# The write of a unit's shifted scores as two transfers of 64 partitions, in a relative-position attention kernel

## The chip, the cores and the metric

The kernel runs on one core of a Trainium2 chip. The metric is the device time of one execution in microseconds. The core has a matrix engine (PE, with its weight loads shown as PEld), a vector engine (DVE), a scalar engine (ACT), a general engine (POOL) and a queue engine (SP) that only issues transfers. ACT issues transfers too. The transfers of both run on the same 16 DMA engines of the core; the profile calls the queue of SP q1 and that of ACT q10.

## The reference

For 16 batches of 512 tokens of width 128 the kernel computes x + attention(LN(x)) + MLP(LN(x)). The attention has 16 heads of width 8 and relative positions; its core, for each batch and head, is:

```
content = einsum(q + u_bias, k)           # 512 x 512 per head
pos     = einsum(q + v_bias, p)           # 512 x 512 per head
# relative shift: a zero column is put ahead, and the rows of 513 are
# read again as rows of 512, from the second row on
padded  = concat([zeros(S, 1), pos])      # 512 x 513
pos     = padded.reshape(S + 1, S)[1:]    # 512 x 512
attn    = softmax((content + pos) * scale)
head    = attn @ v
```

All data are float32. The MLP has three layers with weights of plus and minus one.

## The kernel before

A *unit* is one head of one batch: 256 units. Time is laid out by hand in *halves*, two for each unit. Every engine walks over the same sequence of halves, and semaphores join the engines. The stages of unit u are:

1. Halves 2u to 2u+3: PE multiplies position scores into PSUM (`positions`, L779). ACT copies 128x1024 of them a half into `pos_sb` (L463), whose rows are 513 wide with a zero in the first column. There are four buffers of `pos_sb`.
2. After the copy of half 2u+3, SP writes the unit's `pos_sb` to the DRAM buffer `shift` (L307): 128 partitions of 2052 floats, 1026 KB. This waits for the copies (`s_pe`) and, as there are six buffers of `shift`, for the load of the unit six earlier (`s_in`).
3. At half 2u+8, ACT waits for the write (`s_out_w`, of which there is one for each `pos_sb` buffer) and for a free buffer of `sc_sb`, and issues the load of the same bytes, read from an offset of 512 floats on, into `sc_sb` (L450): this write and read make the relative shift. The wait is in ACT's own sequence. While it is open, the copies and exponentials behind it stand.
4. From half 2u+12, PE multiplies the content scores, DVE adds the loaded shifted scores (L630) and subtracts the row's extreme (L638).
5. From half 2u+17, PE turns the scores (L803) and ACT takes the exponential (L473), then PE multiplies with the values (L817).

The DRAM side of the write is the view `chunks`: element (q, a, c) with 32 q, 4 a and 2052 c; partition p of `pos_sb` holds q = p // 4 and a = p % 4. Between the units' work stand *jobs* (projections, MLP, output), placed by the tables `FRONT`, `MIDDLE` and `BACK`. SP's sequence has, beside one write for each unit, one load of x and one store of the output for each batch. The sequence repeats every 16 units.

Of the kernel before, what the change touches and what calls it, by code (L numbers as in the profile page):

```python
# [11 lines left out]
P = 128  # L12
# [5 lines left out]
def attention_mlp(nc, x, consts, stack_w, wp, pe_t, k0, k1, k2, out):  # L18
# [18 lines left out]
    N_POS = 4  # L37
    N_SC = 6
    N_SHIFT = 6
# [3 lines left out]
    shift = nc.dram_tensor("shift", [N_SHIFT, S * PITCH], F32, kind="Internal").ap()  # L43

    with ExitStack() as ctx:
        def sb(name, shape, dt=F32):
            return ctx.enter_context(nc.sbuf_tensor(name, shape, dt))
# [4 lines left out]
        def sem(name):  # L52
            return ctx.enter_context(nc.semaphore(name))
# [49 lines left out]
        pos_sb = sb("pos_sb", [P, N_POS, NT, PITCH])  # L103
# [47 lines left out]
        s_out_w = [sem(f"s_pout{i}") for i in range(N_POS)]  # L151
# [12 lines left out]
        def wait(eng, s, n):  # L164
            if n > 0:
                eng.wait_ge(s, n)
# [34 lines left out]
        def taken(h):  # L201
            return [j[:3] for j in AT.get(h, []) if j[3] == j[4] - 1]
# [13 lines left out]
        def ev(name, b, c=0):  # L216
            return EV[(name, b, c)] if b >= 0 else 0
# [12 lines left out]
        def unit(n, lag):  # L230
            return n - lag if 0 <= n - lag < UNITS else None

        def half_of(h, lag):
            k = h - lag
            return divmod(k, 2) if 0 <= k < 2 * UNITS else (None, None)

        def blocks(h, lag):

            u, i = divmod(h - lag, 2)
            return [(v, t) for v, t in ((u - 1, i + 2), (u, i)) if 0 <= v < UNITS]  # L240
# [4 lines left out]
        def score_halves(h):  # L245

            return min(max(h + 1, 0), 2 * UNITS + 2)
# [3 lines left out]
        def pt_banks(k):  # L251
            return ps_pos if k >= TWO_PT and (k - TWO_PT) % 2 == 0 else ps_pt
# [16 lines left out]
        def chunks(flat):  # L269

            return flat.rearrange("(a q c) -> q a c", a=4, q=P // 4)
# [6 lines left out]
        @block.sync  # L278
        def _(sp):
            def load_x(b):  # L280
                wait(sp, s_out, 16 * (b - N_X + 1))
                sp.dma_start(x_sb[:, b % N_X].rearrange("p t d -> p (t d)"), chunks(x[b].rearrange("s d -> (s d)"))) \
                  .then_inc(s_x[b % N_X], 16)

            load_x(0)
            sp.dma_start(wp_sb[:, :], wp).then_inc(s_wp, 16)
            sp.dma_start(pe_sb[:, :], pe_t).then_inc(s_enc, 16)
            sp.dma_start(wk, stack_w[:, GROUPS * P:2 * GROUPS * P]).then_inc(s_wk, 16)
            for dst, src in ((k0_u8, k0), (k1_u8, k1), (k2_u8, k2)):
                sp.dma_start(dst, src.rearrange("(a p) n -> p a n", p=P)).then_inc(s_wb, 16)  # L290
            load_x(1)

            for n in STEPS:
                it, slot = n // 16, n % 16
                if it >= 2 and slot == 1:
                    sp.wait_ge(s_jev, ev("TY", it - 2))
                    sp.dma_start(chunks(out[it - 2].rearrange("s d -> (s d)")),
                                 x_sb[:, (it - 2) % N_X].rearrange("p t d -> p (t d)")).then_inc(s_out, 16)
                if 0 <= it and it + 2 < B and slot == 4:
                    load_x(it + 2)  # L300
                u = unit(n, 1)
                if u is not None:
                    sp.wait_ge(s_pe, score_halves(2 * u + 3))
                    if u >= N_SHIFT:
                        v = u - N_SHIFT
                        sp.wait_ge(s_in[v % N_SC], 16 * (v // N_SC + 1))
                    sp.dma_start(chunks(shift[u % N_SHIFT]),  # L307
                                 pos_sb[:, u % N_POS].rearrange("p t c -> p (t c)")) \
                      .then_inc(s_out_w[u % N_POS], 16)
            for k in range(2):  # L310
                sp.wait_ge(s_tail["x"], k + 1)
                sp.dma_start(chunks(out[B - 1].rearrange("s d -> (s d)"))[:, :, 2 * k * D:2 * (k + 1) * D],
                             x_sb[:, (B - 1) % N_X, 2 * k:2 * k + 2, :].rearrange("p t d -> p (t d)")) \
                  .then_inc(s_out, 16)
            sp.wait_ge(s_out, 16 * (B + 1))
# [71 lines left out]
        def _(act):  # L387
# [57 lines left out]
            for h in HALVES:  # L445
                u, i = half_of(h, SHIFT_H)
                if i == 0:
                    act.wait_ge(s_out_w[u % N_POS], 16 * (u // N_POS + 1))
                    wait(act, s_pt, 2 * (u - N_SC + 1))
                    act.dma_start(sc_sb[:, u % N_SC].rearrange("p t c -> p (t c)"),  # L450
                                  chunks(shift[u % N_SHIFT, S:S + S * S])) \
                       .then_inc(s_in[u % N_SC], 16)
                todo = sorted(blocks(h, 0), key=lambda v: v[0] % N_POS)
                if todo:
                    act.wait_ge(s_pos, score_halves(h))
                    for u, t in todo:
                        if t == 0 and u >= N_POS:
                            act.wait_ge(s_out_w[u % N_POS], 16 * (u // N_POS))
                    to = [pos_sb[:, u % N_POS, t, 1:PITCH] for u, t in todo]
                    if len(to) == 2:  # L460
                        to = bass.AP(tensor=to[0].tensor, offset=to[0].offset,
                                     ap=[to[0].ap[0], [to[1].offset - to[0].offset, 2], [1, S]])
                        act.copy(to, ps_pos[:, :, :]).then_inc(s_pe, 1)  # L463
                    else:
                        act.copy(to[0], ps_pos[:, 0, :]).then_inc(s_pe, 1)
                u, i = half_of(h, TURN_H)
                if u is not None:
                    k = 2 * u + i
                    act.wait_ge(s_pt, k + 1)
                    if k == 0:  # L470
                        act.wait_ge(s_wf, 3)
                    wait(act, s_av, k - 1)
                    act.activation(pt_sb[:, 2 * i:2 * i + 2, :], pt_banks(k)[:, :, :], ACT.Exp, scale=-1.0) \  # L473
                       .then_inc(s_exp, 1)
                for j in taken(h):
                    take_job(*j)
                for name, b, c in taken(h - 1):
                    if name == "TZ" and b > 0:
                        act.wait_ge(s_jev, ev("TZ", b))
                        act.copy(z_t[:, :].rearrange("d (a q t) -> d t q a", a=4, t=NT),  # L480
                                 z_q[:, :].rearrange("d (t q a) -> d t q a", a=4, t=NT)).then_inc(s_zt, 1)
# [432 lines left out]
```

## Time and profile before

| | |
|---|---|
| runs | 1458.58, 1460.66, 1461.72 us; median 1460.66 |
| profiled execution | 1460.97 us, of which the span of instructions is 1459.2 us |
| granted clock of PE, mean | 0.999 of full speed |
| bytes moved by DMA | 550.41 MB |

The difference between the execution's time and its span, 1.8 us, lies before the first and after the last instruction. In the section of rows below, a busy time is a sum over instructions. The DMA share is the time in which a packet was open, over the 16 engines; it says little about how much more they could carry, which the GB/s beside it tell better. "To landing" is from the issue of a transfer to its completion.

### The profile page before, as it was taken

Reading aid. Unit: us, or ns where it says so; the run is one execution under the profiler, and the core shown is the slowest. Engines: PE = TensorE matmul, PEld = TensorE weight load, DVE = VectorE, ACT = ScalarE, POOL = GpSimd, SP = SyncE. Lnnn points to the kernel's source line nnn. Section 1 sums busy time; section 2 is a strip of 40 time slices with the busy share of each in tenths; the row PEclk is TensorE's granted clock in tenths of the full one; section 3 lists DMA queues with packets and bytes.
Section 4 is the critical chain, followed back from the end, with each engine's and each line's share of the span. In section 5 each row is a group of like instructions: output and inputs, shape, how many; then the busy total and the mean of one; then the engine's idle time right before and its main releaser. Section 6 shows DMA issues by size and latency. Waiting matters only on the chain.

```text
span 1459.2 us, 41448 instructions
## 1 busy us (share of the span) xinstructions
PE 1444.7 (99%) x16113; PEld 961.4 (66%) x16113; DVE 1335.9 (92%) x3490; ACT 1225.5 (84%) x1364; POOL 726.4 (50%) x721
## 2 busy tenths in 40 slices
PE   8999999999999999999999999999999999999998
PEld 5566666666666666666666666666766666666666
DVE  6899899999999999999998999999899998989996
ACT  5788888888888888888888888888888888888873
POOL 5555455454654556455554555456455554533410
PEclk9999999999999999999999999999999999999999
DMA  5999999999999999999999999999999999999992
GB/s 175 407 397 399 386 391 384 381 394 384 394 381 392 398 383 396 376 391 384 390 397 382 400 384 390 393 375 403 382 391 394 384 398 385 393 381 388 388 403 92
DMA packets 80867, 550.41 MB, mean 377 GB/s; under 512 B 9376, under 2 KB 10528, under 8 KB 15136
## 3 DMA queue, kind: packets, MB, share of 16 engines
q1 hardware_dynamic: 43376, 278.61, 49.3%
q10 hardware_dynamic: 37296, 269.15, 47.9%
q8 instruction: 129, 2.11, 0.6%
q14 instruction: 66, 0.54, 0.1%
HBM read 274.57 MB, written 273.15 MB: 375 GB/s over the span
## 4 chain that ended last, share of the span: by engine, by line
PE 93%; DMA 4%; ACT 2%; DVE 1%; issue 1%; ACTq 0%
PE ps_pt L803 34%; PE ps_av L817 18%; PE ps_pos L779 14%; PE ps_job L706 12%; DMA shift<-pos_sb 4%; PE ps_job L663 3%; PE ps_job L670 3%; PE ps_job L685 2%; ACT pt_sb L473 1%; PE ps_job L681 1%; PE ps_job L693 1%; PE ps_job L676 1%; PE ps_con L791 1%; PE ps_av L655 1%; ACT pos_sb L463 1%
## 5 line engine op out<-in xcount | busy, mean ns | idle before, releaser
L630 DVE CUSTOM_DVE_ANT_0 sc_sb<-ps_con,sc_sb 128x512 f32<-128x512 f32 x1024 | 662.5, 683 | 89.7 <-PE ps_con L791 85.7
L463 ACT COPY pos_sb<-ps_pos 128x1024 f32<-128x1024 f32 x510 | 518.4, 1016 | 190.2 <-PE ps_pos L779 181.1
L638 DVE TENSOR_SCALAR sc_sb<-sc_sb,nmax 128x512 f32<-128x512 f32 x1024 | 604.7, 622 | 0.1
L803 PE MATMUL ps_pt<-c_sb,sc_sb 128*128 128x128 f32 x4048 | 552.5, 279 | 3.4 <-ACT pt_sb L473 2.3
L473 ACT ACTIVATE pt_sb<-ps_pt 128x1024 f32<-128x1024 f32 x506 | 519.5, 1027 | 14.0 <-PE ps_pt L803 13.7
L803 PEld LDWEIGHTS ps_pt<-c_sb,sc_sb 128*128 128x128 f32 x4048 | 433.2, 141 | 128.1 <-issue 96.7
L817 PE MATMUL ps_av<-pt_sb,v_sb 128*9 128x128 f32 x8192 | 319.9, 274 | 0.6 <-ACT pt_sb L473 0.6
L817 PEld LDWEIGHTS ps_av<-pt_sb,v_sb 128*9 128x9 f32 x8192 | 172.8, 90 | 208.3 <-issue 205.5
L366 POOL CAST h<-act_sb 128x512 fp32r<-128x512 f32 x128 | 83.0, 649 | 390.8 <-ACT act_sb L439 390.4
L791 PE MATMUL ps_con<-k_stack,q_stack 26*128 26x512 f32 x1024 | 261.9, 496 | 0.1
L779 PE MATMUL ps_pos<-p_stack,q_stack 26*128 26x512 f32 x1024 | 258.5, 496 | 3.4 <-ACT pos_sb L463 3.0
L706 PE MATMUL ps_job<-h,w 128*128 128x512 f32 x640 | 188.9, 417 | 0.0
L779 PEld LDWEIGHTS ps_pos<-p_stack,q_stack 26*128 26x128 f32 x1024 | 96.7, 181 | 118.4 <-issue 110.8
L367 POOL TENSOR_TENSOR h<-act_sb,h 128x512 fp32r<-128x512 f32 x128 | 164.3, 1283 | 10.4
L357 POOL TENSOR_TENSOR k_stack<-act_sb,c_sb 128x512 fp32r<-128x512 f32 x63 | 70.4, 1118 | 122.3 <-ACT act_sb L434 122.3
L357 POOL TENSOR_TENSOR q_stack<-act_sb,c_sb 128x512 fp32r<-128x512 f32 x62 | 69.5, 1122 | 114.7 <-ACT act_sb L434 114.0
L706 PEld LDWEIGHTS ps_job<-h,w 128*128 128x128 f32 x640 | 108.6, 190 | 15.2 <-ACT act_sb L434 0.2
L791 PEld LDWEIGHTS ps_con<-k_stack,q_stack 26*128 26x128 f32 x1024 | 98.4, 181 | 4.1 <-DVE nmax L630 2.4
L439 ACT ACTIVATE act_sb<-ps_job,col 128x512 f32<-128x512 f32 x128 | 87.8, 686 | 1.8 <-PE ps_job L706 1.7
L358 POOL TENSOR_TENSOR k_stack<-act_sb,k_stack 128x512 fp32r<-128x512 f32 x63 | 80.6, 1279 | 4.9
L630 DVE DVE_READ_ACCUMULATOR2_ANT nmax<- 128x1 f32 x1024 | 81.9, 80 | 0.0
L358 POOL TENSOR_TENSOR q_stack<-act_sb,q_stack 128x512 fp32r<-128x512 f32 x62 | 79.4, 1281 | 4.9
(109 smaller groups left out, 983.2 us busy)
## 6 DMA issues: line engine op xcount, KB each, us to landing
shift<-pos_sb SPq DMA_DIRECT2D x256, 1026.0 KB, 9.2
sc_sb<-shift ACTq DMA_DIRECT2D x256, 1024.0 KB, 9.9
x_sb<-in_x SPq DMA_DIRECT2D x16, 256.0 KB, 10.9
out<-x_sb SPq DMA_DIRECT2D x15, 256.0 KB, 10.1
c_sb<-in_consts ACTq DMA_DIRECT2D x1, 288.0 KB, 6.9
o_t<-in_wp SPq DMA_DIRECT2D x1, 256.0 KB, 5.5
stack_w_sb<-in_stack_w ACTq DMA_DIRECT2D x1, 256.0 KB, 5.1
heads<-in_pe_t SPq DMA_DIRECT2D x1, 256.0 KB, 6.6
```

What stands on the lines that cost most here:

```text
L357: own(pool.tensor_tensor(dst, src, low.broadcast_to([P, S]), ALU.mult))
L358: pool.tensor_tensor(dst, src, dst.bitcast(F32), ALU.subtract).then_inc(s_hl, 1)
L367: pool.tensor_tensor(dst[:, 1, :], src, dst[:, 0, :].bitcast(F32), ALU.subtract) \
L463: act.copy(to, ps_pos[:, :, :]).then_inc(s_pe, 1)
L473: act.activation(pt_sb[:, 2 * i:2 * i + 2, :], pt_banks(k)[:, :, :], ACT.Exp, scale=-1.0) \
L630: dve.tensor_tensor_reduce(sc_sb[:, m % N_SC, t, :], ps_con[:, k, :], sc_sb[:, m % N_SC, t, :], -SCALE, 3.4e38, ALU.add, ALU.min, nmax[:, ...
L638: dve.tensor_scalar(sc_sb[:, m % N_SC, t, :], sc_sb[:, m % N_SC, t, :], nmax[:, m % N_SC, t:t + 1], None, ALU.subtract).then_inc(s_sub, 1)
L706: return pe.matmul(ps_job[:, :], lhs, src[:, a, hl, :], start=(a == 0 and hl == 0), stop=(a == len(before) - 1 and hl == 1))
L779: ins = pe.matmul(ps_pos[:, bank, :], QS[rows, g, t * P:(t + 1) * P], PS[rows, g, :], start=True, stop=True)
L791: pe.matmul(ps_con[:, bank, :], QS[rows, g, t * P:(t + 1) * P], KS[rows, g, :], start=True, stop=True).then_inc(s_con, 1)
L803: last = pe.transpose(pt_banks(k)[:, j % 2, t * P:(t + 1) * P], sc_sb[:, u % N_SC, t, j * P:(j + 1) * P], id_sb)
L817: last = pe.matmul(ps_av[32 * t:32 * t + DH + 1, h % 4, :], v_sb[:, b % 2, j, h, :], pt_sb[:, j, t * P:(t + 1) * P], start=(j == 0), stop= ...
```

## The change

SP issues two transfers for a unit where there was one. The first takes partitions 0 to 63 of `pos_sb` to the first 16 of 32 q of the DRAM view, the second partitions 64 to 127 to the other 16. The bytes and their places are the same. Both add 16 to the same semaphore, so the two waits of ACT on it (ahead of the load, and ahead of the reuse of a `pos_sb` buffer) ask for 32 for each use.

```diff
                         sp.wait_ge(s_in[v % N_SC], 16 * (v // N_SC + 1))
-                    sp.dma_start(chunks(shift[u % N_SHIFT]),
-                                 pos_sb[:, u % N_POS].rearrange("p t c -> p (t c)")) \
-                      .then_inc(s_out_w[u % N_POS], 16)
+                    for k in range(2):
+                        sp.dma_start(chunks(shift[u % N_SHIFT])[P // 8 * k:P // 8 * (k + 1)],
+                                     pos_sb[P // 2 * k:P // 2 * (k + 1), u % N_POS].rearrange("p t c -> p (t c)")) \
+                          .then_inc(s_out_w[u % N_POS], 16)
...
-                    act.wait_ge(s_out_w[u % N_POS], 16 * (u // N_POS + 1))
+                    act.wait_ge(s_out_w[u % N_POS], 32 * (u // N_POS + 1))
...
-                            act.wait_ge(s_out_w[u % N_POS], 16 * (u // N_POS))
+                            act.wait_ge(s_out_w[u % N_POS], 32 * (u // N_POS))
```

SP's queue, at the place in the first third of a batch where a store of the output and a load of x stand between the writes; before (`s_pe` is ACT's copies, `s_in` the load of six units earlier, `s_jev` and `s_out` belong to the output):

```order
L307 DMA shift<-pos_sb 32x4x2052 [waits s_in1,s_pe]
L297 DMA out<-x_sb 32x4x512 [waits s_jev]
L307 DMA shift<-pos_sb 32x4x2052 [waits s_in2,s_pe]
L307 DMA shift<-pos_sb 32x4x2052 [waits s_in3,s_pe]
L307 DMA shift<-pos_sb 32x4x2052 [waits s_in4,s_pe]
L282 DMA x_sb<-in_x 128x1x512 [waits s_out]
```

The same place of the changed kernel:

```order
L308 DMA shift<-pos_sb 16x4x2052 [waits s_in1,s_pe]
L308 DMA shift<-pos_sb 16x4x2052
L297 DMA out<-x_sb 32x4x512 [waits s_jev]
L308 DMA shift<-pos_sb 16x4x2052 [waits s_in2,s_pe]
L308 DMA shift<-pos_sb 16x4x2052
L308 DMA shift<-pos_sb 16x4x2052 [waits s_in3,s_pe]
L308 DMA shift<-pos_sb 16x4x2052
L308 DMA shift<-pos_sb 16x4x2052 [waits s_in4,s_pe]
L308 DMA shift<-pos_sb 16x4x2052
L282 DMA x_sb<-in_x 128x1x512 [waits s_out]
```

Each write has become two with half the q, the second of which waits for nothing; no other transfer has changed its place between units. ACT's sequence in the middle of a batch, where it waits for the writes (`s_pout2` is the `s_out_w` of one `pos_sb` buffer), before:

```order
L450 DMA sc_sb<-shift 128x1x2048 [waits s_pt,s_pout2]
L463 COPY pos_sb<-ps_pos 128x2x512 [waits s_pout2,s_pos]
L473 ACTIVATE pt_sb<-ps_pt 128x1024 [waits s_av,s_pt]
L463 COPY pos_sb<-ps_pos 128x2x512 [waits s_pos]
L473 ACTIVATE pt_sb<-ps_pt 128x1024 [waits s_av,s_pt]
```

And of the changed kernel:

```order
L451 DMA sc_sb<-shift 128x1x2048 [waits s_pt,s_pout2]
L464 COPY pos_sb<-ps_pos 128x2x512 [waits s_pout2,s_pos]
L474 ACTIVATE pt_sb<-ps_pt 128x1024 [waits s_av,s_pt]
L464 COPY pos_sb<-ps_pos 128x2x512 [waits s_pos]
L474 ACTIVATE pt_sb<-ps_pt 128x1024 [waits s_av,s_pt]
```

Only the line numbers and the counts that are waited for have moved. The orders of PE, DVE and POOL are the same as well.

## Rows read from the trace of the kernel before

**Rows 1.** Page, part 1: busy time and share of each engine.

```profile
PE 1444.7 (99%) x16113; PEld 961.4 (66%) x16113; DVE 1335.9 (92%) x3490; ACT 1225.5 (84%) x1364; POOL 726.4 (50%) x721
```

**Rows 2.** Page, part 4: the chain that ended last, by engine.

```profile
PE 93%; DMA 4%; ACT 2%; DVE 1%; issue 1%; ACTq 0%
```

**Rows 3.** Windows of three batches: length, busy (count), clock, DMA share, GB/s.

```profile
1077.14:1165.01 87.87, 87.87 (x1007) 58.75 (x1004) 81.98 (x216) 76.37 (x85) 47.14 (x47) 1.00 1.01 387
1165.01:1252.88 87.87, 87.87 (x1006) 58.75 (x1004) 82.00 (x216) 76.37 (x85) 47.19 (x47) 1.00 1.01 393
1252.88:1340.74 87.86, 87.86 (x1004) 58.74 (x1004) 81.60 (x208) 76.37 (x85) 39.72 (x38) 1.00 1.01 386
```

**Rows 4.** Waits of the SP queue: us in total, times, longest.

```profile
SPq L307 <- ACT pos_sb L463: 1234.4, 255, 13.4
```

**Rows 5.** Waits of all engines, whole span.

```profile
ACT pos_sb L463 <- PE ps_pos L779: 181.1, 366, 1.2
...
ACT pos_sb L463 <- DMA shift<-pos_sb: 3.2, 1, 3.2
...
DVE sc_sb L630 <- DMA sc_sb<-shift: 2.9, 3, 1.4
```

**Rows 6.** Chain in order of time, its long DMA pieces: start us, us, what.

```profile
34.47 11.25 DMA shift<-pos_sb
...
206.68 13.53 DMA shift<-pos_sb
...
295.07 13.74 DMA shift<-pos_sb
...
647.95 13.65 DMA shift<-pos_sb
```

**Rows 7.** DMA issues: KB each, median us to landing.

```profile
shift<-pos_sb SPq DMA_DIRECT2D x256, 1026.0 KB, 9.2
sc_sb<-shift ACTq DMA_DIRECT2D x256, 1024.0 KB, 9.9
...
out<-x_sb SPq DMA_DIRECT2D x2, 128.0 KB, 2.1
```

**Rows 8.** Line L307, window 60 to 1400: issue durations in ns, landing.

```profile
L307 SPq DMA_DIRECT2D shift<-pos_sb x244: 517/518/532, 60.6 to 1396.3; - x122
...
DMA to landing us min/median/max: 6.7/9.2/13.7
```

**Rows 9.** Line L307, window 19 to 22: the first write, alone.

```profile
L307 SPq DMA_DIRECT2D shift<-pos_sb x1: 587/587/587, 20.1 to 20.1; - x1
...
DMA to landing us min/median/max: 4.4/4.4/4.4
```

**Rows 10.** Line L307, window 704 to 706: a write in mid-run.

```profile
L307 SPq DMA_DIRECT2D shift<-pos_sb x1: 517/517/517, 704.6 to 704.6; - x1
...
DMA to landing us min/median/max: 9.2/9.2/9.2
```

**Rows 11.** Timeline of ACT: that write's load is issued.

```profile
716.18 0.52 ACTq L450 DMA_DIRECT2D sc_sb<-shift  x1
```

**Rows 12.** Timeline of ACT around 220 us.

```profile
220.23 0.52 ACTq L450 DMA_DIRECT2D sc_sb<-shift  x1
220.85 1.02 ACT L463 COPY pos_sb<-ps_pos 128x1024 f32<-128x1024 f32 x1 [1.44 <-PE ps_pt L803]
```

**Rows 13.** Window 34 to 60, columns as in rows 3.

```profile
34.00:60.00 26.00, 22.86 (x117) 12.74 (x116) 20.99 (x51) 16.47 (x20) 15.35 (x15) 0.93 1.01 405
```

**Rows 14.** Line L307, window 1415 to 1416: the last write.

```profile
DMA to landing us min/median/max: 11.0/11.0/11.0
```

**Rows 15.** Line L450, window 1426 to 1428: its load.

```profile
L450 ACTq DMA_DIRECT2D sc_sb<-shift x1: 521/521/521, 1426.5 to 1426.5; - x1
```

**Rows 16.** Page, part 3: packets, MB and share of each queue.

```profile
q1 hardware_dynamic: 43376, 278.61, 49.3%
q10 hardware_dynamic: 37296, 269.15, 47.9%
```

## The prediction, made before the changed kernel was run

> **What bounds the kernel now.** I read the share of each engine first [rows 1]: PE is busy for 99% of the span, DVE for 92%, ACT for 84%. The chain that ended last [rows 2] is 93% PE and 4% DMA. Windows laid over three batches [rows 3] agree: 87.87 us each, of which PE works 87.87 us at full clock. That is 5.49 us for each of 16 units. So in mid-run PE is the bound, and a change on a transfer can only save what is lost outside of such batches.
>
> Then the transfers, since the change is one of them. SP has time: it waits 1234 us in all, 255 times, for ACT's copies [rows 4], and an issue takes it 0.52 us [rows 8]. The transfer itself has little. The write of a unit is issued after the copy of half 2u+3 and must have landed when ACT comes to half 2u+8. In mid-run it was issued at 704.6 and landed 9.2 us later, at 713.8 [rows 10]. ACT issued the load at 716.18 [rows 11], so 2.4 us were left. The landing times reach from 6.7 to 13.7 us [rows 8], and the slack is often gone. Of the 256 pairs of a write and its load, worked out in this way, 31 have the load within 0.3 us of the write's landing. The first is the write issued at 34.47 with a landing of 11.25 us [rows 6], the last the one at 1415.4, which landed after 11.0 us and whose load went out at 1426.5 [rows 14, 15]. 47 pairs have under 1 us, 100 under 2 us. Most of the short ones cost nothing yet, since ACT has about 0.7 us of idle time a unit (181.1 us of waits for PE [rows 5], over 256). Four are on the chain [rows 6]: the one at 34.47, where ACT's next copy stood 3.2 us for it [rows 5], and three of 13.5 to 13.7 us. At the one that landed at 220.2, ACT's copy had been idle for 1.44 us [rows 12], about 1 us more than usual.
>
> Why a write takes 9.2 us is told by comparing it with one that is alone. The first write landed in 4.4 us [rows 9]; one of 128 KB at the end takes 2.1 us [rows 7]. The difference, 898 KB in 2.3 us, is 400 GB/s. So the bytes of one write stream for 2.63 us, and some 1.8 us are fixed. In mid-run a write and a load share the engines. How near are these to their limit? In the stretch of 34 to 60 us, where ACT was waiting for writes and PE was idle for 3 us, they moved 405 GB/s [rows 13]; in the PE-bound batches 387 to 393 [rows 3], 389 in the mean. 389 GB/s over 5.49 us is 2.13 MB for a unit; at 405 GB/s this takes 5.27 us, which is just two times 2.63. **The DMA engines would bound the kernel at 5.27 us a unit, and PE does at 5.49: the cover is 0.22 us, 4%.**
>
> **The change, part by part.**
>
> *One more issue for each unit.* 256 more instructions on SP, each 0.52 us [rows 8]. SP is idle 1234 us of 1459, so SP itself is not late. The second half starts some 0.55 us after the first. With one more write or load still on the queues, as is the rule (9.2 us to land against a unit's 5.49), the engines have the first half to move meanwhile (1.3 us at full rate), so this costs nothing in mid-run. For a write that finds the engines idle it costs up to 0.5 us; only the first two do, and neither is waited for. The out store and the x load behind the writes are 0.55 us later, with a batch's time to spare. Zero.
>
> *16 more completion packets a unit.* q1 has 43376 packets, q10 37296 [rows 16]. For 256 writes this fits 128 packets of data and 16 of completion each. The change makes that 128 + 32, and the queue's total 47472. What a completion packet costs is not seen by itself. The backlog's 405 GB/s, which carries two sets of completions a unit, is no lower than the 400 GB/s that come from data alone, so the lower bound is nothing. For the upper bound I give all of the fixed 1.8 us to the completions of a transfer and let no other packet pass meanwhile, which no row suggests: 1.8 us a unit. I take 0, nearer to the two equal rates.
>
> *Each transfer touches 64 partitions.* This is where the price lies. The first write shows a transfer that reads all 128 partitions: 400 GB/s. No row has a transfer of 64. If the paths by which the DMA engines reach the on-chip memory are spread over the partitions, half of the partitions offer half of the paths, and with one half read after the other, the unit's write streams for 2.63 f us, where f is between 1 (the path is no limit) and 2 (it always is). With f = 2 the write alone takes 5.26 us, with the load's 2.63 behind it 7.9 us. But f falls where engines alternate between a write packet and a load packet: two engines that share a path collide only while both are at a write. In perfect alternation f is 1, with chance phases about 1.4. I take f = 1.2, the middle of these two, as nearer to the only rows there are, in which a write and a load run side by side without loss (2 x 2.63 = 5.27). A unit then needs 2.63 + 2.63 x 1.2 = 5.79 us on the DMA engines. This is above PE's 5.49: **the bound moves from PE to DMA, and each unit is 0.30 us longer**. The break-even is f = 1.09.
>
> The Trainium skill speaks on this. Its page "SBUF — State Buffer", section "Door 1: The DMA port swizzle", says that partitions 0 to 63 reach only 8 of 16 ports, and gives 196 GB/s for them at 1 MiB against 328 for all 128. By these figures an estimate for a unit's write is 5.4 us against 3.2, f = 1.7, if nothing of it were hidden behind the load. No run here shows a half transfer; the trace agrees as far as 128 partitions alone ran above what the page gives for 8 ports. The page "DMA: Bandwidth & Descriptors", section "Rules for kernel authors", advises against this very split, as the halves run one after the other.
>
> *The counts of 32.* They make ACT wait for both halves, so nothing is released sooner. Zero.
>
> **Sum.** The own time of the profiled execution is 1460.97 us. From 60 to 1400 us there are 244 units [rows 8]: 244 x 0.30 = +73. The stretch of 34 to 60 us, already held by DMA, has 5 units at +0.53 = +2.6. The three steps of about 1 us at the late writes go up in the new period, -3. Total +73, or 1534 us. The execution lies 0.3 us above the median of the runs shown, which is nothing here.
>
> **The rivals.**
>
> *DMA latency rises, but PE stays the bound.* If f is below 1.09, the transfers still fit, with 0 to 0.2 us of cover left, and writes land perhaps 0.5 to 1 us later. For it: 47 pairs have under 1 us. Against a large price: ACT's idle 0.7 us a unit takes up most overruns. Some ten more stalls of 1 to 1.5 us, +4 to +15: about 1470 us.
>
> *Hidden altogether.* If all 16 engines read the halves at full rate and the second issue stands behind the first, writes land as before. For it: SP's idle time, the backlog. Against: it needs both the path and the completions free with 4% to spare. 1461 us, within 3.
>
> *Faster.* Mechanism: with two shorter transfers each engine's part is in smaller runs, and if the first half's fixed 1.8 us passes under the second's streaming, the last byte lands earlier by a part of it. It decides if the landing falls by about 1 us: then the write at 34.47 no longer holds ACT's copy (-3.2 us) and the three mid-run steps go (-3). More cannot be had, since the batches are PE's. 1455 us. Against it: the fixed time is paid after the last byte, which no split moves forward, and the last half is issued later.
>
> *The rule of the ports in full.* f at chance phases or above, 1.4: 6.31 us a unit, +0.82 x 244 = +200: 1660 us. For it are the first page's figures only; in the rows nothing. It lies at the end of the first case.
>
> **How the numbers follow.** DMA becomes the bound: 0.47, its own range 1475 to 1640 (f from 1.1 to 1.37). Latency only: 0.20. Hidden: 0.18. Faster: 0.15. A measurement of this kernel can tell about 0.2% (3 us) from no change. Slower by more: 0.47 + 0.19 = 0.66; same: 0.01 + 0.17 + 0.02 = 0.20; faster: 0.01 + 0.13 = 0.14. The range for 8 in 10 must take in both signs: 1457 leaves out most of the faster case, 1610 the cases of f above 1.32.
>
> **What would show it.** In the changed kernel's profile: the first write, alone, lands after 6 us or more instead of 4.4 if half the partitions mean half the rate; after 5.0 if only the second issue counts. The landing of the halves' second in mid-run goes from 9.2 to above 11 us. Batches are longer than 87.87 us with PE idle, the long pieces of the write stand all along the chain, and the waits gain a large row of ACT's copy for the write. GB/s falls to about 370 with the engines' share still at 1.0. SP's idle time stays above 1000 us. I am wrong if the batches keep their 87.87 us and landings their median.

## The result, and the profile of the changed kernel

The changed kernel takes 1479.49 us (1477.79 to 1481.75), the kernel before 1461.19 us on the same chip: a ratio of 1.013, with a 95% interval of 1.0108 to 1.0151. It is slower, as forecast, but by 18 us and not by 73. The profiled execution took 1481.08 us with a span of 1479.2 us. One execution of one kernel further down ("More time before ACT's wait", with one transfer) ran at a granted clock of 0.556 and took 2377 us; it is left out of every time given here.

Page of the changed kernel: busy time by engine, then the chain by engine, then two rows of the transfers.

```profile
PE 1450.8 (98%) x16113; PEld 964.5 (65%) x16113; DVE 1338.6 (90%) x3490; ACT 1224.2 (83%) x1364; POOL 722.6 (49%) x721
...
q1 hardware_dynamic: 47472, 278.63, 49.9%
...
PE 87%; DMA 8%; ACT 2%; DVE 1%; issue 1%; SPq 0%; ACTq 0%
...
sc_sb<-shift ACTq DMA_DIRECT2D x256, 1024.0 KB, 10.4
```

The engines do the same work as in [rows 1]. On the chain DMA has 8% instead of 4% [rows 2]. The packets of SP's queue are the 47472 that were forecast, against [rows 16].

Windows of 88 us through the first part of the run (length, busy times, clock, DMA share, GB/s):

```profile
60.00:148.00 88.00, 87.01 (x987) 57.40 (x986) 79.28 (x208) 75.82 (x84) 46.52 (x46) 0.99 0.99 382
148.00:236.00 88.00, 85.62 (x979) 57.05 (x976) 80.17 (x207) 74.28 (x83) 44.27 (x44) 1.00 1.00 381
236.00:324.00 88.00, 86.74 (x982) 58.07 (x981) 81.20 (x214) 75.05 (x85) 45.14 (x46) 1.00 1.00 383
324.00:412.00 88.00, 88.00 (x1008) 58.78 (x1010) 82.17 (x216) 76.28 (x86) 46.56 (x47) 1.00 1.01 389
412.00:500.00 88.00, 85.05 (x957) 56.57 (x956) 78.00 (x203) 72.01 (x81) 42.63 (x43) 0.98 1.00 372
500.00:588.00 88.00, 88.00 (x1011) 58.73 (x1002) 82.10 (x216) 76.48 (x86) 46.83 (x46) 1.00 1.00 388
```

This is the row that the forecast got wrong. Some windows are still wholly PE's, at 388 and 389 GB/s as in [rows 3]. Others lack 1 to 3 us of PE. So the period did not become longer everywhere; it is broken at single places. The prediction named the opposite as its sign: batches longer throughout and about 370 GB/s. The lowest of these windows has 372, the undisturbed ones 388 and 389. The chain names them, to be read against [rows 6]:

```profile
37.38 10.68 DMA shift<-pos_sb
...
197.04 13.83 DMA shift<-pos_sb
...
287.39 12.72 DMA shift<-pos_sb
...
465.55 13.74 DMA shift<-pos_sb
...
645.31 12.29 DMA shift<-pos_sb
...
749.90 13.27 DMA shift<-pos_sb
...
1000.40 12.89 DMA shift<-pos_sb
...
1178.22 12.95 DMA shift<-pos_sb
...
1410.65 11.42 DMA shift<-pos_sb
```

Nine where there were four. Six of the seven that lie in mid-run (all but the one at 749.90) are the write that SP issues next after a batch's output store; the seventh stands behind the load of x. From 60 us on, the 14 writes behind an output store land after 12.6 us in the mean, where the kernel before has 9.9; the 221 writes with neither the store nor the load of x directly ahead take 10.8 against 9.3. So the late ones come about once a batch, where a 256 KB store shares the queue.

The waits say the same; before it was 3.2 us, once [rows 5]. First all engines, then SP's queue, where 1234.4 us [rows 4] have become 1010.3:

```profile
ACT pos_sb L464 <- DMA shift<-pos_sb: 18.2, 9, 3.6
```

```profile
SPq L308 <- ACT pos_sb L464: 1010.3, 255, 14.5
```

The largest of these steps, on ACT's timeline (the load is issued at 479.31, 2.6 us after ACT was free, and the copy behind it had stood for 3.21 us):

```profile
476.04 0.68 ACT L440 ACTIVATE act_sb<-ps_job,col 128x512 f32<-128x512 f32 x1
479.31 0.52 ACTq L451 DMA_DIRECT2D sc_sb<-shift  x1
479.93 1.01 ACT L464 COPY pos_sb<-ps_pos 128x1024 f32<-128x1024 f32 x1 [3.21 <-DMA shift<-pos_sb]
```

Paired one by one, a unit's write (from the first issue to the landing of the last half) takes 10.9 us in the mean against 9.4, and its load 10.4 against 9.9. The median of the write is 10.8; the prediction's sign was above 11. The time left before ACT issues the load has fallen from a median of 2.2 us to 0.9, and pairs with under 0.3 us are 73 instead of 31. (Both halves count on one semaphore, so the landing given for a first half can be made up of completions of the second. With a tiny transfer on the same semaphore, an experiment below, the whole write seemed to land at a median of 7.0 us instead of 9.2. Only the last landing of a unit is used here.)

Where the 20 us of the span arise follows from the times at which the write of the same unit is first issued in the two traces. At unit 0 the changed kernel is 0.7 us late, which has nothing to do with the change; at unit 8 it is 5.6 us late and at unit 32 as well; at 64, 128, 192 and 255 it is 7.8, 12.5, 16.5 and 19.9 us late. So 5 us are lost in the start, up to 60 us, and 14 us in mid-run, in steps of up to 5 us.

The traces also record every packet. A write's packet is 8208 bytes. In the first write, which is alone, it is open for 470 ns in the mean against 315 before. From 324 to 1200 us it is open for 344 ns against 337, and a packet of the load for 335 against 339. Each engine carries 8 of both kinds a unit, which makes 5.43 us of open time against 5.41. So alone the packets of a half get in each other's way, and in the mixed stream hardly anything of it shows in their times.

### The profile page after: what moved, and what is told of

Its sections match the earlier page's. It is cut to its first block, busy times and chain, and to the rows that moved or that the text cites. A ratio compares the mean times of both kernels' runs of the same rounds, so it can differ in the third digit from the quotient of the medians.

```text
span 1479.2 us, 41704 instructions
## 1 busy us (share of the span) xinstructions
PE 1450.8 (98%) x16113; PEld 964.5 (65%) x16113; DVE 1338.6 (90%) x3490; ACT 1224.2 (83%) x1364; POOL 722.6 (49%) x721
## 3 DMA queue, kind: packets, MB, share of 16 engines
q1 hardware_dynamic: 47472, 278.63, 49.9%
## 4 chain that ended last, share of the span: by engine, by line
PE 87%; DMA 8%; ACT 2%; DVE 1%; issue 1%; SPq 0%; ACTq 0%
PE ps_pt L804 32%; PE ps_av L818 17%; PE ps_pos L780 13%; PE ps_job L707 11%; DMA shift<-pos_sb 8%; PE ps_job L671 4%; PE ps_job L664 3%; ACT pt_sb L474 1%; PE ps_job L686 1%; PE ps_job L682 1%; PE ps_job L694 1%; PE ps_job L677 1%; ACT pos_sb L464 1%; PE ps_av L656 1%; PE ps_con L792 1%
## 5 line engine op out<-in xcount | busy, mean ns | idle before, releaser
L780 PE MATMUL ps_pos<-p_stack,q_stack 26*128 26x512 f32 x1024 | 259.2, 496 | 12.6 <-ACT pos_sb L464 12.2
L368 POOL TENSOR_TENSOR h<-act_sb,h 128x512 fp32r<-128x512 f32 x128 | 164.6, 1286 | 10.4
## 6 DMA issues: line engine op xcount, KB each, us to landing
sc_sb<-shift ACTq DMA_DIRECT2D x256, 1024.0 KB, 10.4
```

The lines of the kernel that those rows point to most:

```text
L368: pool.tensor_tensor(dst[:, 1, :], src, dst[:, 0, :].bitcast(F32), ALU.subtract) \
L780: ins = pe.matmul(ps_pos[:, bank, :], QS[rows, g, t * P:(t + 1) * P], PS[rows, g, :], start=True, stop=True)
```

## The experiments

All ratios are to the kernel before on the same chip, with 95% intervals. **Theory A**: a transfer that covers a contiguous half of the partitions reaches memory by fewer paths. **Theory B**: the second issue and the completions cost the time.

**Even and odd partitions.**

```diff
-                        sp.dma_start(chunks(shift[u % N_SHIFT])[P // 8 * k:P // 8 * (k + 1)],
-                                     pos_sb[P // 2 * k:P // 2 * (k + 1), u % N_POS].rearrange("p t c -> p (t c)")) \
+                        sp.dma_start(chunks(shift[u % N_SHIFT])[:, k::2, :],
+                                     pos_sb[k::2, u % N_POS].rearrange("p t c -> p (t c)")) \
```

> Two transfers of 64 partitions for each unit as in the changed kernel, but the first takes the even partitions and the second the odd ones (32 q of 2 a). Issues, packets, their sizes and completions are those of the changed kernel. Theory A (a contiguous half of the partitions is reached by fewer paths): the cost goes away, 1461 within 4 us, mid-run landing of a unit's write back near 9.4 us, first unit's write alone landed about 5.0 us after its first issue instead of 6.0. Theory B (the second issue and the 16 more completions cost it): the time stays at 1479 within 4 us, and the first write still takes about 6.0 us.

Measured: 1459.2 us, ratio 0.9989 (0.9980 to 0.9998). The first unit's write, alone, in this kernel:

```profile
L308 SPq DMA_DIRECT2D shift<-pos_sb x2: 589/594/599, 19.9 to 20.6; - x2
...
DMA to landing us min/median/max: 3.1/3.5/3.8
```

and in the changed kernel:

```profile
L308 SPq DMA_DIRECT2D shift<-pos_sb x2: 590/592/595, 20.8 to 21.4; - x2
...
DMA to landing us min/median/max: 4.4/4.9/5.4
```

Even and odd: 20.6 + 3.8 = 24.4, which is 4.5 us after the first issue, as fast as the one transfer of [rows 9]. Contiguous halves: 21.4 + 5.4 = 26.8, 6.0 us. Issues, packets and completions are equal, and a packet of the even/odd kernel's first write is open for 315 ns, as in the kernel before. So the cost lies in which partitions and rows a half takes, as theory A has it, and theory B falls. Each half still has 64 partitions: it is not their number that costs. Paired, the mid-run write takes 9.6 us. The edit changes the DRAM side too, which the next two kernels take apart.

**Which side of the transfer?** Two mirrored kernels: one has the DRAM view of the even/odd kernel with the on-chip view of the changed one, the other the reverse. In both the rows of `shift` are permuted, so the scores are other numbers; nothing else is left out.

```diff
-                        sp.dma_start(chunks(shift[u % N_SHIFT])[P // 8 * k:P // 8 * (k + 1)],
+                        sp.dma_start(chunks(shift[u % N_SHIFT])[:, k::2, :],
```

```diff
-                                     pos_sb[P // 2 * k:P // 2 * (k + 1), u % N_POS].rearrange("p t c -> p (t c)")) \
+                                     pos_sb[k::2, u % N_POS].rearrange("p t c -> p (t c)")) \
```

> On-chip side as in the changed kernel (partitions 0 to 63, then 64 to 127), DRAM side as in the even/odd kernel (32 q of 2 a). The rows of shift are permuted by this, so the scores are other numbers; nothing else is left out. Theory A1 (the on-chip partitions' paths cost it): as the changed kernel, 1475 to 1482 us. Theory A2 (the DRAM side of the halves costs it): 1459 to 1462 us.

> The mirror of the run before: on-chip side even and odd partitions, DRAM side as in the changed kernel (16 q of 4 a, then the other 16), again with permuted rows. Theory A1: 1458 to 1462 us. Theory A2: 1475 to 1482 us.

Measured: contiguous on chip alone 1481.36 us, ratio 1.0115 (1.0066 to 1.0164), in the range of the changed kernel's 1.013. Contiguous in DRAM alone 1474.58 us, ratio 1.0045 (1.0016 to 1.0073); on this chip the kernel before took 1466.0 us, and the ratio is what counts. (The first one's trace is of its slowest execution, 1487.17 us of 1478.23 to 1487.17.) Waits of ACT's copy for the write, of the first, then of the second:

```profile
ACT pos_sb L464 <- DMA shift<-pos_sb: 29.4, 17, 3.4
```

```profile
ACT pos_sb L464 <- DMA shift<-pos_sb: 14.0, 8, 3.0
```

The first unit's write, alone, of the first and of the second:

```profile
L308 SPq DMA_DIRECT2D shift<-pos_sb x2: 588/593/598, 20.3 to 20.9; - x2
...
DMA to landing us min/median/max: 4.4/5.1/5.8
```

```profile
L308 SPq DMA_DIRECT2D shift<-pos_sb x2: 583/589/595, 20.2 to 20.9; - x2
...
DMA to landing us min/median/max: 4.1/4.4/4.8
```

That is 6.4 us for contiguous halves on chip alone and 5.4 us (5.38 before rounding) for contiguous halves in DRAM alone, against 4.5 for even and odd on both sides and 6.0 for contiguous on both. The mean time for which a packet of it is open is 549, 417, 315 and 470 ns in the same order. So the on-chip side carries most of the time lost, but the second kernel is far from free: it was expected to cost nothing, costs 0.45%, and its paired writes in mid-run land after 10.9 us in the mean, as late as the changed kernel's. Either the DRAM side has a price, or the other pairing of partitions with rows has one; no run separates these. It also shows that the mean landing does not fix the loss: with the same 10.9 us, 89 of its pairs have under 0.3 us, and it loses a third as much.

**One tiny transfer more.**

```diff
                       .then_inc(s_out_w[u % N_POS], 16)
+                    sp.dma_start(spare[u % N_POS], pos_sb[0:16, u % N_POS, 0, 0:16]) \
+                      .then_inc(s_out_w[u % N_POS], 16)
```

> The kernel before with one more transfer behind each write, 16 partitions of 16 floats into a spare buffer, on the same semaphore (so ACT waits for 32 as in the changed kernel): one more issue and 16 more completions a unit, next to no bytes. The big write is whole. Theory A: 1461 to 1465 us. Theory B: near 1479 us, and the landing of a unit's writes up by 1.5 us as in the changed kernel.

Measured: 1466.8 us, ratio 1.0041 (1.0017 to 1.0065). So an issue, 16 packets of 64 bytes and 16 completions behind the whole write cost 6 us, more than nothing. From the write's issue to the tiny transfer's landing it is 10.4 us in the mean, 0.9 above the kernel before. They are last on the queue and ACT waits for them:

```profile
ACT pos_sb L466 <- DMA spare<-pos_sb: 10.0, 6, 1.9
```

The even/odd kernel has as many and loses nothing, so this is not a third of the changed kernel's loss that could be added up.

**Halves of the columns.**

```diff
+                        sp.dma_start(chunks(shift[u % N_SHIFT])[:, :, 2 * PITCH * k:2 * PITCH * (k + 1)],
+                                     pos_sb[:, u % N_POS, 2 * k:2 * k + 2].rearrange("p t c -> p (t c)")) \
```

> Two transfers of all 128 partitions and half the columns (1026 floats each): the same issues and completions a unit as the changed kernel, twice the data packets at half the size (4104 bytes). Theory A: 1461 to 1466 us, the rest above the kernel before being the price of 128 more packets a unit. Theory B: 1479 or more.

Measured: 1665.25 us, ratio 1.1375 (1.1324 to 1.1426). Theory A's 1461 to 1466 is missed, and theory B's "1479 or more" is met in form only: the even/odd kernel has the same issues and completions and loses nothing. A second experiment cuts the load in the same way (and its two waits ask for 32).

```diff
-                    act.dma_start(sc_sb[:, u % N_SC].rearrange("p t c -> p (t c)"),
-                                  chunks(shift[u % N_SHIFT, S:S + S * S])) \
+                    for k in range(2):
+                        act.dma_start(sc_sb[:, u % N_SC, 2 * k:2 * k + 2].rearrange("p t c -> p (t c)"),
+                                      chunks(shift[u % N_SHIFT, S:S + S * S])[:, :, 2 * k * S:2 * (k + 1) * S]) \
```

> The column kernel, which took 1665 us, with the load cut into two column halves as well, so that the packets of the two queues are again about equal (4104 and 4096 bytes). If the write starved because the engines serve the two queues packet by packet and its packets were half as long, the time falls back towards 1470 us. If packets of 4104 bytes to DRAM rows cost the engines themselves, it stays at 1665 us or grows.

Measured: 1596.66 us, ratio 1.0926 (1.0874 to 1.0977). One window of each (500 to 675.7 us), first of the column kernel, then with both cut:

```profile
500.00:675.70 175.70, 157.84 (x1754) 103.67 (x1750) 151.10 (x381) 129.81 (x149) 79.99 (x80) 0.99 1.02 343
```

```profile
500.00:675.70 175.70, 164.30 (x1848) 108.91 (x1847) 152.94 (x396) 136.95 (x157) 81.16 (x83) 0.99 1.05 358
```

This lies between the two outcomes that were expected. Still more packets made it faster, so a part of the first loss was, most likely, the unequal packets of the two queues. But with the engines open all the time both stay at 343 and 358 GB/s, so packets of 4.1 KB cost the engines themselves as well. How much of this is the size and how much that two transfers now write each 8208-byte row of DRAM is open.

**Less computation, so that the transfers bound it.** Three kernels.

```diff
-                return [lambda a=a, hl=hl: product(a, hl) for a in range(len(before)) for hl in range(2)]
+                return [lambda a=a, hl=hl: product(a, hl) for a in range(len(before)) for hl in range(2)
+                        if (a, hl) == (0, 0) or a == len(before) - 1]
...
-                for j in (2 * i, 2 * i + 1):
+                for j in (2 * i,):
...
+                    part = slice(0, S if k == 0 else 64)
-                    dve.tensor_scalar(sc_sb[:, m % N_SC, t, :], sc_sb[:, m % N_SC, t, :],
+                    dve.tensor_scalar(sc_sb[:, m % N_SC, t, part], sc_sb[:, m % N_SC, t, part],
```

> Kernel before with less computation, so that PE needs some 4.6 us a unit, ACT 4.8 and DVE 4.2: 5 of 8 products of each MLP layer-1 and layer-2 job, half of the value matmuls and 7/8 of every second subtraction are left out. All transfers stand. The DMA engines should be the bound: 5.27 us a unit by the backlog's rate, about 1405 us in all, GB/s 405, writes waited for throughout.

> The same omissions in the changed kernel. Its period a unit is the DMA engines' own need with contiguous halves, 2.63 (1 + f). The prediction's f = 1.2 gives 5.79 us. Since the changed kernel lost only 18 us in all, f near 1.06 to 1.09 is as well possible: 5.42 to 5.5 us. If the halves cost latency only and no rate, the period is that of the light kernel before, within 0.05 us.

> The same omissions with even and odd partitions as the two transfers. Theory A (paths): the period of the light kernel before within 0.05 us. Theory B (issues and completions): that of the light changed kernel.

Measured: 1434.04 us (1426.86 and 1441.23), 1453.64 us (eight executions, 1445.45 to 1459.20) and 1438.08 us (1433.97 and 1442.20). The middle window (675.7 to 851.4) of one transfer, and of contiguous halves:

```profile
675.70:851.40 175.70, 163.68 (x1491) 101.43 (x1491) 161.84 (x443) 154.98 (x176) 94.43 (x97) 0.99 1.01 403
```

```profile
675.70:851.40 175.70, 160.34 (x1447) 99.19 (x1446) 157.41 (x432) 149.63 (x171) 91.14 (x92) 0.99 1.01 394
```

Over three such windows each, the means are 397, 390 and 398 GB/s. With 2.13 MB a unit these are periods of 5.37, 5.47 and 5.36 us. Contiguous halves cost 0.10 us a unit here: f = 1 + 0.10 / 2.63 = 1.04, where the prediction had 1.2. Two things make this an estimate only. The traces are of the fastest execution of the first kernel and of the slowest of the second, and by the medians the difference is 20 us over 256 units, 0.08 us a unit with the start's loss in it, or f = 1.03. And the light kernels are not held by DMA alone (25% of the first one's chain, 31% of the second's), so the engines' own need can have grown by more than the period. The packets speak against much more: in mid-run those of the two queues are open for 340 + 333 ns against 331 + 333, 0.07 us a unit. The light kernel with one transfer also did not reach the 1405 us that I expected of it.

**The load cut to a quarter** (the buffer it fills is set to zero at the start).

```diff
-                    act.dma_start(sc_sb[:, u % N_SC].rearrange("p t c -> p (t c)"),
-                                  chunks(shift[u % N_SHIFT, S:S + S * S])) \
+                    act.dma_start(sc_sb[:, u % N_SC].rearrange("p t c -> p (t c)")[:, 0:512],
+                                  chunks(shift[u % N_SHIFT, S:S + S * S])[:, :, 0:512]) \
```

> The kernel before with the load of shifted scores cut to a quarter (512 of 2048 floats of each partition; the rest of the scores stays what it was, and a memset of that buffer at the start adds some us). With little to share the engines with, a write in mid-run should land near what it takes alone: 4.5 to 5 us.

> The same cut in the changed kernel. If the two halves collide with themselves on the paths and are only spared by the alternation with the load's packets, a unit's write now takes about 6 us from the first issue, 1.5 us above the run before, as it does for the first unit, and yet the total is that of the run before within 3 us, since ACT comes for it 11 us after the issue. If instead the load makes the conflict, the difference of the landings shrinks to the 0.6 us of the second issue.

Measured: 1469.14 and 1468.27 us. First the kernel with one transfer, its writes from 60 to 1400 us and a window (the DMA share is the last figure but one); then the same of the halves, with one unit in mid-run:

```profile
DMA to landing us min/median/max: 4.7/5.0/6.5
```

```profile
500.00:675.70 175.70, 175.70 (x2005) 117.49 (x2004) 164.01 (x431) 152.63 (x171) 93.15 (x93) 1.00 0.75 247
```

```profile
L308 SPq DMA_DIRECT2D shift<-pos_sb x2: 518/556/595, 574.1 to 574.6; - x2
...
DMA to landing us min/median/max: 4.9/5.5/6.2
```

```profile
500.00:675.70 175.70, 175.70 (x2007) 117.47 (x2005) 164.15 (x431) 152.71 (x171) 93.31 (x93) 1.00 0.90 247
```

One write lands after 5.0 us; two halves end at 574.6 + 6.2 = 580.8, 6.7 us after 574.1 (median over the run 6.9). For the same 247 GB/s the engines have packets open for 0.90 of the time instead of 0.75. So the halves do collide with themselves, in mid-run too, and with time to spare (4.7 us in the median before the load is issued) this costs the total nothing. The rise of 1.9 us was expected as 1.5.

**More time before ACT's wait.**

```diff
-    SHIFT_H = 8
-    CONTENT_LAG = 6
+    SHIFT_H = 9
+    CONTENT_LAG = 7
...
-    N_POS = 4
+    N_POS = 5
```

> The kernel before with one more half for the write and one more for the load: SHIFT_H 9 instead of 8, CONTENT_LAG 7 instead of 6, five pos_sb buffers instead of four, the last batch's two closing jobs two halves later. To make room, three of four blocks of the MLP's second hidden layer share one place (its numbers are other ones; all instructions stand). A write has about 2.8 us more until ACT waits for it. Before has four such waits on its chain, worth about 6 us; the longer pipeline costs 5.5 us at the end. Some 1460 us, no chain piece of the write in mid-run.

> The same in the changed kernel. Theory A with the price paid at ACT's wait (the halves cost latency and little rate): the loss is gone, the time is that of the run before within 3 us, with landings still 1.5 us above its. If the halves cost rate beyond PE's 5.49 us a unit, the loss stays: about 18 us above the run before.

Measured: 1566.65 and 1573.23 us. Both miss the expected time by 100 us: in the new order PE itself needs 5.9 us a unit (98% of the second kernel's chain), so it is no better kernel. Room for the fifth buffer was made by letting three blocks of the MLP's second hidden layer share one place, and the last batch's closing jobs are two halves later. What it does show: all waits of the second for the write, 5.4 us in two, lie before 60 us, none later, and the halves cost it 6.6 us, about what they cost the changed kernel in its start. That is more than the 3 us expected; that it arises in the start is read from the second kernel's waits alone. Its waits for the two transfers:

```profile
ACT pos_sb L465 <- DMA shift<-pos_sb: 5.4, 2, 3.3
DVE sc_sb L632 <- DMA sc_sb<-shift: 5.0, 1, 5.0
```

The transfers also run at a lower rate here (361 GB/s in mid-run), so more time and less load together took the mid-run loss away; which of the two did it is not separated.

## Why the prediction was right in direction and wrong in size

**The bound before** was read rightly. PE holds the batches, the DMA engines have a few per cent to spare, and the write's landing is the thin place.

**Each transfer touches 64 partitions**: half right. The halves do slow each other, and the first write alone needs 6.0 us, which was the sign named for it. But the reason given was that half of the partitions offer half of the paths, and the even/odd kernel also has 64 partitions a transfer and loses nothing. What costs is the contiguous half, on chip most, and on the DRAM side or by the pairing too (5.4 us alone), which the prediction did not consider. That fewer paths are behind it remains an inference from longer packets (470 against 315 ns); no run shows the paths.

**The step that failed is the value f = 1.2**, and with it "the bound moves from PE to DMA, and each unit is 0.30 us longer". It was the middle between perfect alternation (1) and chance phases (1.4), and neither 1.4 nor the choice of the middle came from a row. In the light kernels it is about 1.03 to 1.04, and the packets of the changed kernel itself are open for only 0.02 us more a unit, which as an estimate is 1.01; all are below the break-even of 1.09 that the text itself gave. Alone, f is (6.0 - 1.8) / 2.63 = 1.6, so the collisions are strong when a write has the engines to itself, and nearly gone in rate where a load runs beside it. The +73 of 244 equal units was therefore no term at all. (The case's own lower end was also off: f = 1.1 gives 5.52 us, which is +8 and 1469 us, not 1475. And its "rule of the ports in full", 1660 us, lies outside its range and got no chance.) In its place stands what the first rival described, with a larger price: landings 1.5 us later, nine late writes on the chain instead of four, 14 us in mid-run. The measured 1479.49 us falls into the range of the favoured case by number, 1475 to 1640, but not by its mechanism. I gave this rival 0.20 and +4 to +15 us, the price too low because I let ACT's 0.7 us of idle time absorb most overruns. It does at 64 of the 73 pairs without slack; the other nine cost up to 5 us each. What the prediction left out is where they come: it treated all units alike, and six of the seven in mid-run stand behind the batch's output store, where a write now takes 12.6 us. PE then stands as well, and in the window from 412 to 500 its mean granted clock is 0.98.

**The start** had +2.6 us for the stretch already held by DMA. It is about 5 us. The even/odd kernel also loses 1.6 us there, so not all of it is the contiguous halves.

**One more issue for each unit** was put at nothing, at 0.52 us each. It is not quite that. Issues of the changed kernel last up to 2.5 us in mid-run. At the worst late write the first half's issue took 1.18 us, behind an output store whose issue took 2.87:

```profile
459.74 2.87 SPq L297 DMA_DIRECT2D out<-x_sb  x1
```

```profile
L308 SPq DMA_DIRECT2D shift<-pos_sb x1: 1184/1184/1184, 464.3 to 464.3; - x1
```

SP has time for this in general, but there it came on top of a landing of 13.7 us. It is not the rule: in five of the seven late writes of mid-run the second half was issued 0.56 us after the first, and in two 1.1 to 1.2 us after. With the load cut to a quarter, issues last up to 2.6 us and nothing is lost. So long issues are not the main cause; whether they add something at those two is not separated.

**The completions** at nothing: borne out by the even/odd kernel and by the packets (a completion is open for 9 ns), though a tiny transfer at the end of the queue is not free (+6 us).

**The counts of 32** and the orders of the other engines: as forecast, nothing. **Faster** did not occur for the changed kernel. For even and odd partitions the ratio's interval ends just below 1; by the 0.2% bound it is no change, and no run here that does all the work beats the kernel before by more.

## What to carry to other kernels

When a transfer is split, split it so that each part still spans the partitions evenly, let both sides of it take the same rows, and keep its packets long. The half that is contiguous in partitions took 6.0 us instead of 4.4 alone, the half in columns cost 14%, the even/odd one nothing. And when a resource with 4% to spare gets 2% more work, do not multiply a longer period by all units: pair each issue with its landing, see how the slack is distributed, and look at what else stands in the queue where it is short.

## What the runs showed of the hardware that was not expected

- Two transfers of all partitions with packets of 4104 bytes instead of one with 8208 took the rate in mid-run from 386 to 393 GB/s down to 332 to 343 with the engines open throughout, and shortening the other queue's packets as well brought some of it back (358 to 360 GB/s).
- A DMA's partitions may be strided on the on-chip side (every second one) at no cost: 4.5 us alone for two such halves, 4.4 us for the one transfer. That holds with the DRAM rows that belong to these partitions; the same partitions written to the first half of the DRAM view took 5.4 us.
- The packets of two contiguous halves are open 1.5 times as long when they are alone (470 against 315 ns), and hardly longer with an equal stream of loads beside them (344 against 337 ns). Beside a load of a quarter it is 513 against 362 ns.
- The issue of a write by SP, 517 to 532 ns throughout in mid-run of the kernel before, lasts up to 2490 ns with two contiguous halves a unit and up to 1574 ns with even and odd ones.
